# A two-layer token model on one core: gate products and bias rows placed between sums of gathered rows, and blocks of the last layer turned in three of four tiles

## The reference, cut to what matters

```python
logits1 = xt @ g1
v1, i1 = jax.lax.top_k(logits1, TOP_K_L1)          # 2 of 8 groups
w1 = softmax(v1)
c1 = sum(one_hot(i1, G) * w1[..., None], axis=1)
logits2 = einsum('td,gde->tge', xt, g2)
v2, i2 = jax.lax.top_k(logits2, TOP_K_L2)          # 2 of 8 experts in each group
c2 = sum(one_hot(i2, E) * softmax(v2)[..., None], axis=2)
h = relu(einsum('td,gedh->tgeh', xt, W1) + b1)     # 256 hidden
y = einsum('tgeh,gehd->tged', h, W2) + b2
out = einsum('tgd,tg->td', einsum('tged,tge->tgd', y, c2), c1)
return hidden + out
```

## Time and profile before

| | us |
|---|---|
| median of 3 runs | 1264.49 |
| lowest and highest of them | 1263.4, 1265.91 |
| the profiled execution's own time | 1261.42 |
| its span in the profile | 1259.6 |
| PE busy | 809.0 |
| DVE busy | 780.4 |
| POOL busy | 539.8 |
| ACT busy | 443.5 |

### The profile page before, as it was taken

One profiled execution on the slowest core, in us unless ns is written; L12 is line 12 of the kernel. 1 busy time (PEld: TensorE's weight loads), 2 busy tenths in 40 slices (PEclk: granted clock), 3 DMA queues, 4 the chain that ended last, 5 costly groups with the idle time before them and its releaser, 6 DMA issues.

```text
span 1259.6 us, 17773 instructions
## 1 busy us (share of the span) xinstructions
PE 809.0 (64%) x5133; PEld 648.9 (52%) x5133; DVE 780.4 (62%) x2295; ACT 443.5 (35%) x1251; POOL 539.8 (43%) x564
## 2 busy tenths in 40 slices
PE   0206965769999248778687313487777888888530
PEld 0205355559999124434255302376666777777420
DVE  6896274756665238888767799555555546665532
ACT  2274150514444133433103307433333444444100
POOL 7863000245440644662101006766666325554366
PEclk9657975559999556666665555589999999999555
DMA  2390049102221267567400404033333223332222
GB/s 69 119 378 1 1 142 321 79 26 71 71 68 43 57 130 137 121 137 137 76 0 1 128 0 138 26 83 88 87 84 88 79 68 89 89 95 84 55 62 61
DMA packets 116601, 112.94 MB, mean 90 GB/s; under 512 B 16404, under 2 KB 102995, under 8 KB 116259
## 3 DMA queue, kind: packets, MB, share of 16 engines
q1 hardware_dynamic: 103228, 84.68, 24.7%
q0 software_dynamic: 13280, 27.13, 8.3%
HBM read 76.15 MB, written 35.57 MB: 89 GB/s over the span
## 4 chain that ended last, share of the span: by engine, by line
PE 54%; DVE 26%; issue 9%; ACT 4%; POOL 3%; DMA 2%; another core or an unknown queue 2%; SPq 1%; DVEq 0%; POOLq 0%; ACTq 0%
PE ps L601 17%; PE ps L608 15%; DVE wide L1304 6%; PE ps L1880 4%; POOL wide L840 3%; DVE bnst L921 2%; DVE wide L1189 2%; PE ps L596 2%; PE ps L2140 2%; PE ps L2050 2%; PE ps L2091 2%; PE ps L2030 1%; ACT wide L1678 1%; DVE mv L924 1%
## 5 line engine op out<-in xcount | busy, mean ns | idle before, releaser
L601 PE MATMUL ps<-wide 128*128 (+1 forms) x1580 | 247.7, 288 | 42.1 <-issue 23.9
L608 PE MATMUL ps<-big,wide 128*128 x1568 | 237.9, 282 | 31.9 <-ACT wide L568 18.0
L833 POOL DMA_INDIRECT wide<-xrows,holder x189 | 182.0, 963 | 138.3 <-PE ps L596 93.9
L601 PEld LDWEIGHTS ps<-wide 128*128 128x128 f32 x1580 | 208.1, 196 | 59.8 <-issue 55.9
L608 PEld LDWEIGHTS ps<-big,wide 128*128 128x128 f32 x1568 | 205.0, 195 | 39.5 <-issue 39.2
L518 DVE TENSOR_SCALAR wide<-ps,wide 128x128 f32<-128x128 f32 x395 | 131.5, 348 | 133.6 <-PE ps L601 119.3
L568 ACT ACTIVATE wide<-ps,wide 128x128 f32<-128x128 f32 x395 | 138.0, 368 | 191.0 <-PE ps L601 173.2
L840 POOL DMA_INDIRECT wide<-results,place x128 | 128.0, 1000 | 129.5 <-DVE h L1284 61.1
L1304 DVE TENSOR_REDUCE wide<-ps 125x3 f32<-125x1500 f32 (+1 forms) x96 | 143.8, 1540 | 46.5 <-PE ps L1880 44.1
L1880 PE MATMUL ps<-big 97*125 97x500 bf16 x256 | 105.3, 547 | 39.3 <-DVE wide L1304 33.0
L586 ACT COPY wide<-ps 128x128 f32<-128x128 f32 x322 | 85.6, 266 | 117.8 <-PE ps L608 100.9
(11 more groups left out here) (370 smaller groups left out, 1156.7 us busy)
## 6 DMA issues: line engine op xcount, KB each, us to landing
results<-wide SPq DMA_DIRECT2D x161, 128.0 KB, 1.8
big<-kappa SPq DMA_DIRECT2D x8, 1750.0 KB, 20.7
big<-parts SPq DMA_DIRECT2D x96, 125.0 KB
big<-in_L_ffn_W_dram SPq DMA_DIRECT2D x10, 1024.0 KB, 8.5
big<-in_L_ffn_W_dram SPq DMA_DIRECT2D x64, 128.0 KB, 2.6
parts<-wide SPq DMA_DIRECT2D x24, 250.0 KB
xrows<-wide SPq DMA_DIRECT2D x2, 1792.0 KB
wide<-results,place POOLq DMA_INDIRECT x192
```

What stands on the lines that cost most here:

```text
L601: last = t.matmul(ps[:, (2 if k < c.HC // 2 else 4) + u % 2, 128 * k:128 * k + 128], ring.w1[u % U][:, 128 * k:128 * k + 128], turned, sta ...
L608: last = t.matmul(ps[:, 6 + u % 2, 0:D], ring.hid[u % 2][:, 128 * k:128 * k + 128], w[:, D * k:D * k + D], start=k == 0, stop=k == c.HC - 1)
L833: gp.indirect_dma_start(ring.rows[j % RING], None, xrows[:, :], bass.IndirectOffsetOnAxis(ap=holder[:, j:j + 1], axis=0)).then_inc(S(f"row ...
```

## The change

Two things change.

First, in the last layer the blocks 0 to 78 are turned as before, block n in tile n-2, but the blocks 79 to 125 in three of four tiles: tile 79, 80, 81, then 83, 84, 85, and so on up to tile 140. `turn_at` holds which tile turns which block. The loops over tiles are written with one rule for all tiles. PE's turn now also waits for the copy of the block two before, and every tile waits for the blocks it needs (`blocks_for`) and for its weights. DVE's copy now goes to an address known when the program is built, not to one in a register.

Second, `late_gates` is cut into seven steps, which stand after the picks 80, 82, ..., 92, and the eight `add_bias` stand after the picks 100, 103, ..., 121.

```diff
+        self.turn_at = {self.turn_tile(n): n for n in range(2, self.blocks)}
+    def turn_tile(self, n):
+        extra = n - self.part_blocks[0]
+        return n - 2 if extra < 0 else self.part_blocks[0] - 2 - -4 * (extra + 1) // 3
+    def blocks_for(self, tile):
+        ends = 0
+        for i, blocks in enumerate(self.part_blocks):
+            ends += blocks
+            if tile < ends + (i + 1) * (self.E - 1):
+                return min(ends, tile - i * (self.E - 1) + 1)
...
+BIAS_AT = 20
...
-                    if u < turns:
-                        pe.wait_ge(S(f"row_ld{(u + 2) % RING}"), ...)
-                        turn(u + 2)
-                        pe.wait_ge(S(p + "blocks_in"), first_tile + (u + 2))
-                    if u >= turns:
-                        pe.wait_ge(S(p + "w1_ready"), first_tile + (u + 4))
+                    if first_tile + u in c.turn_at:
+                        n = c.turn_at[first_tile + u]
+                        pe.wait_ge(S(f"row_ld{n % RING}"), 16 * (n // RING) + 16 + earlier_rows(c, n))
+                        pe.wait_ge(S(p + "blocks_in"), n - 1)
+                        turn(n)
+                    if first_tile + u + 1 < c.tiles:
+                        pe.wait_ge(S(p + "blocks_in"), c.blocks_for(first_tile + u + 1))
+                    pe.wait_ge(S(p + "w1_ready"), first_tile + (u + 4))
...
-                    for n in range(inside, FIRST_PICKS):
+                    for n in range(inside, 16 * B):
                         combine_pick(n)
-                    late_gates()
-                    dve.wait_ge(S("f1_combined"), FIRST_PICKS)
-                    for b in range(SPLIT + 1):
-                        add_bias(f, b)
-                    for n in range(FIRST_PICKS, 16 * B):
-                        ...
+                        step = n - FIRST_PICKS
+                        if step in range(0, 14, 2):
+                            late_gates(step // 2)
+                        if step in range(BIAS_AT, BIAS_AT + 3 * B, 3):
+                            dve.wait_ge(S("f1_combined"), n + 1)
+                            b = (step - BIAS_AT) // 3
+                            add_bias(f, b)
                             wait_evac(dve, f"bias{f}", b)
-                        combine_pick(n)
```

More of the change, by code:

```diff
@@ L58, in __init__ @@
         self.tab = self.tiles + 4 if n else self.tiles + 10
-        self.full = (self.blocks - 2) // RING
+        self.turn_at = {self.turn_tile(n): n for n in range(2, self.blocks)}
         self.banks = self.E * NT // 512 or 1
@@ L510, in stage, with turn @@
                 v.tensor_copy(ring.w1[u % U], w1v[:, bass.ds(w1, c.wcols)]).then_inc(S(p + "w1_ready"), 1)
-            def turn(u, kept):
-                v.tensor_copy(ring.blocks[:, bass.ds(kept, 128)], ps[:, u % 2, 0:128]).then_inc(S(p + "blocks_in"), 1)
+            def turn(n):
+                kept = 128 * (n % KEEP[c.n])
+                v.tensor_copy(ring.blocks[:, kept:kept + 128], ps[:, n % 2, 0:128]).then_inc(S(p + "blocks_in"), 1)
             def rectify(u):
@@ L536, in expert_vector, with tiles @@
             rectify(0)
-            def tiles(first_tile, count, turns):
+            def tiles(first_tile, count):
                 for u in range(count):
-                    if u < turns:
-                        dve.wait_ge(S(p + "turned"), first_tile + (u + 3))
-                        turn(u, words.value(u, 1))
+                    if first_tile + u in c.turn_at:
+                        n = c.turn_at[first_tile + u]
+                        dve.wait_ge(S(p + "turned"), n + 1)
+                        turn(n)
                     dve.wait_ge(S(p + "hid_filled"), first_tile + (u + 4))
@@ L550, in tiles @@
                         combine_pick(n - n // COMBINE_STEP - 1)
-            for i in range(c.full):
-                tiles(i * RING, RING, RING)
-            tiles(c.full * RING, RING, c.blocks - 2 - c.full * RING)
-            if c.tiles // RING > c.full + 1:
-                for i in range(c.full + 1, c.tiles // RING):
-                    tiles(i * RING, RING, 0)
-            tiles(c.tiles // RING * RING, c.tiles % RING, 0)
+            for i in range(0, c.tiles, RING):
+                tiles(i, min(RING, c.tiles - i))
             words.free()
@@ L1199, in _, with late_gates @@
             TT, TS = v.tensor_tensor, v.tensor_scalar
-            def late_gates():
+            def late_gates(step):
                 m = mask_views(1)
```

43 lines of the change are left out of this document (21 added, 22 removed).

## The result

The changed kernel takes 1249.39 us (median of 4 runs, 1246.72 to 1251.82) beside 1264.43 us for the kernel before (4 runs): a ratio of 0.9887, 95% interval 0.9871 to 0.9903. It is faster by 1.1%, some 15 us. I had forecast 24.5 us. The profiled execution took 1246.72 us with a span of 1244.9, against 1261.42 and 1259.6 before: 14.7 us in the span.

A forecast was written before the change was run, and what follows sets the result against it. The tail was taken as bound by POOL's gathers, the tiles as slowed by a stall; 17.5 us (tail) + 7.0 (tiles) = 24.5 off the profiled 1261.4 makes 1236.9, plus 3.1 to the median: 1240.0 us, range 1231 to 1250.

The forecast's parts named there:

- rival 1: Tiles: the stall follows the gathers three by three, spreading turns gives nothing; 17.5 us gained, 1247.0 us; chance 0.22.
- Two of the signs that I had named: Tail: the forecast is wrong if POOL waits for picks over 2 us at a time, or bias rows hold DVE.
- Pick 80 no longer waits, 19.0 us: Tail: pick 80 right behind pick 79 frees gather 88's place, so POOL's excess wait of 19.0 us goes.
- The gathers' loss beside the gates, 1.5 us more than before: Tail: gathers beside DVE's gate operations lose 1.5 us more than the present 4.16; bounds 0 to 6.6 more.
- rival 3: Tail: every gate operation stops POOL in full; 12.4 + 7.0 = 19.4 us gained, 1245.1 us; chance 0.13.
- DVE keeps up: Tail: DVE's 34 us of work fits a stretch of over 60; falling 1.5 us behind stays hidden under 7.5 us.
- The bias rows are in time: Tail: row 0 is ready 3.7 us before it is asked for; lateness up to 3.7 + 7.5 us would not show.
- The 3.7 us interval holds beside gathers: Tail: bias rows come every 3.7 us whether or not gathers run beside them; the argument against late rows.
- rival 4: Tiles: broken turn stream makes PE stall for each gather, 48.6 us more less 17.5, 1295.6 us; chance 0.03.
- The tiles, 7.0 us: Tiles 77 to 140: spread turns give rounds like the picks' tiles, 1.31 us per tile, 79.7 instead of 86.7 us.
- The end stays: End of the tail: the time from gather 127 on does not change.
- Rival 5: Tail: bias rows over 11 us late hold DVE and POOL, so no difference within the noise; chance 0.03.

The follow-up runs named there:

- `turns_only`: The changed kernel with the new turning order but gates and bias rows in one piece as in the kernel before: 1259.72 us, ratio 0.9984 to the kernel before.
- `depth4`: Kernel before with only the new tail, POOL four gathers ahead instead of eight in the last layer, on the faster chip: 1165.74 us, ratio 0.9904.

## Why the prediction was wrong

The 1249.4 us lie just inside the wide range (1231 to 1250) and nearest to rival 1 (1247.0), but that is luck: rival 1 had 17.5 us in the tail and nothing in the tiles, the trace has 12.4 and 2.3. Two of the signs that I had named came: POOL waits 4.46 us for a pick, and bias rows hold DVE. By its own steps:

- **Pick 80 no longer waits, 19.0 us.** Right. The wait is gone, and from gather 80 to 96 POOL runs as I described.
- **The gathers' loss beside the gates, 1.5 us more than before.** Too much: they lost 4.2 us, as before (4.16). The 512-wide operations cost 0.3 us together, and a wide one costs 1.2 to 1.5 us. The trace agrees here with the rule of the Trainium skill, page "SBUF — State Buffer", section "SBUF: two separate sides", which I had weighed against my rate: a gather waits for the operation to end, by the three ends above. What rival 3 made of it, every operation stopping POOL in full, didn't come, because a good part of each operation lies in the time between two gathers.
- **DVE keeps up.** Right: it waited for gathers, apart from the bias rows.
- **The bias rows are in time.** This is the step that failed. The first three came even sooner than I had worked out (first add possible at 1194.7), 3.70 us apart. The next two were held up; row 4's copy came at 1222.95 instead of 1192.03 + 4 x 3.70 = 1206.83, 16.1 us late. The row that DVE stood for was row 3: at 3.70 us a row from 1194.7 it could have been added at 1205.8 and was at 1222.29, 16.5 us late. I had written that up to 11.2 us would not show and each further one would be one of the result; the wait of POOL in excess is 4.2 us, near 16.5 - 11.2 = 5.3. What I had no account of is the end: the rest of the chain comes at 3.70 to 4.66 us a row from 1222.95 on and outlasts the gathers, 2.6 us. Together the hold-up costs 6.7 us, and the tail gives 12.4 net instead of 17.5.
- **The 3.7 us interval holds beside gathers.** This was my evidence, and it was weak. In the trace before, six of the eight rows are made while POOL stands still, and a gather stream as long as the new one never lay beside the chain. The forecast had seen the sign, late signals "once for three gathers" in the tiles and 3.12 us beside eight gathers, and priced it there alone, in rival 4, not for the chain that the change moves beside 48 gathers.
- **The tiles, 7.0 us.** The mechanism was named right and sized wrong: `turns_only` gives 2.4 us by its median (0 to 4 by its interval), the trace here 2.3, the traces beside `turns_only` 3.7 to 5.6. The nearest row, the picks' tiles, has another kind of gather; with row gathers the rounds took 5.48 us on average for 5.24, the longest 6.15, and the nine tiles behind them 1.08 each for 1.03. The rounds are near the 5.6 of rival 1, that spreading gives nothing.
- **The end stays.** Wrong by the 2.6 us above.

In sum 12.4 + 2.3 = 14.7, the span's difference (the 1.7 us ahead of the change and the -1.6 of the picks' tiles cancel). Rival 5 had the mechanism in part (bias rows over 11 us late hold POOL), but not its size: the gain shrinks and doesn't vanish.

What is shown: the hold-up comes with back-to-back gathers and goes with pauses, by nothing else than two memsets behind every fourth gather. That the forecast would have come out without it was not shown: the pauses that remove it cost as much as it does, and the changed kernel did not run on the chip without it. What stays open: what in the chip holds the signals; whether the gaps or the mean pace of the gathers count; why one of the five chips of the experiments doesn't do it; whether SP's stores lengthen it; and whether the tiles' stalls are the same thing. They are absent on the same chip, but one memset behind each gather, 0.14 us, did not remove them; two behind each gather of the tiles ran only on the chip that has no stalls. A kernel without the stores was not run.

## What to carry to other kernels

When a chain of small steps that hand over between engines is moved beside a long stream of gathers from GpSimd, its pace measured elsewhere is no evidence; look in the trace for steps whose producer has long finished while the waiter idles ("remote", or several engines going on at once), and price the chain by them. A cover (here 11.2 us) is to be weighed against the longest such hold-up and not against jitter. And a pause of 0.6 us in the stream can take such a wait away, but it is not free: seven of them cost here what they saved, and that four are cheaper is likely and not shown.

## What the runs showed of the hardware

- ACT saw PE's finished turn 12.6 us late, and DVE PE's finished product 12.9 us late, while GpSimd issued gathers every 1.25 us. Every version with this chain beside an unbroken stream of gathers, eight ahead, had a wait of 15.7 to 19.8 us in it on chips of that kind. In the changed kernel signals still passed at 1199.4, seven gathers after the last long one; a gap of 0.6 us more behind every fourth gather removed it all, one of 0.13 us more didn't.
- A 128x64 memset on GpSimd that is waited for adds 0.13 us to the gathers' step of 1.25, two add 0.62.
- The kernel before takes 1177 us on one chip and 1254 to 1264 on the others. The mean granted clock is no reason: 0.755 in `depth4` there, and 0.755 in the kernel before here. On that chip a round of picks takes 4.18 us for 5.30, eight gathers ahead on both.
- A 2048-wide addition or product on DVE stopped a gather that fell into it until 0.81 us after its end (three of three in the changed kernel).
